# The carry of a recurrent scan kept in fp32, its low part subtracted from SBUF alone

## What is computed

```python
def res_step(prev, xt):
    new = jnp.tanh(xt + prev @ W_res.T)          # W_res is 256 x 256
    new = LEAK * new + (1.0 - LEAK) * prev       # LEAK = 0.95
    return (new, new)
_, res_states = jax.lax.scan(res_step, h0, xin)  # h0: (8 batches, 256)
```

## Time and profile before

| | us |
|---|---|
| median of 3 runs | 635.62 (635.25 to 636.78) |
| the profiled execution: its own time | 634.58 |
| its span, first to last instruction | 632.8 |
| busy: TensorE matmul / VectorE / ScalarE / POOL | 596.5 / 549.2 / 456.4 / 190.8 |

### The profile page before, as it was taken

How to read it: one execution, slowest core, us unless ns; L and a number is a source line. 1 busy time by engine, 2 the same in 40 slices (tenths; PEclk the granted TensorE clock), 3 DMA queues, 4 the chain that set the end, 5 groups by cost and what they waited for, 6 DMA issues and landing times.

```text
span 632.8 us, 28184 instructions
## 1 busy us (share of the span) xinstructions
PE 596.5 (94%) x11015; PEld 475.9 (75%) x11015; DVE 549.2 (87%) x2334; ACT 456.4 (72%) x2244; POOL 190.8 (30%) x427
## 2 busy tenths in 40 slices
PE   7888888999999999999999999999999999999973
PEld 2554454888888888888888888888889888888762
DVE  5789996899888889998999999999777799899985
ACT  5687796677777777777777777777757677677664
POOL 1555364000000000010000000000000488888886
PEclk9999999999999999999999999999999999999997
DMA  6000000000000000000000000000030000000001
GB/s 212 2 2 1 2 1 2 4 4 2 4 4 4 4 3 4 4 4 3 4 4 4 4 2 4 4 4 4 3 70 3 3 18 18 19 16 18 16 20 30
DMA packets 8629, 8.30 MB, mean 13 GB/s; under 512 B 944, under 2 KB 7088, under 8 KB 8496
## 3 DMA queue, kind: packets, MB, share of 16 engines
q1 hardware_dynamic: 8208, 5.51, 3.2%
q10 hardware_dynamic: 288, 0.99, 0.5%
HBM read 3.35 MB, written 2.10 MB: 9 GB/s over the span
## 4 chain that ended last, share of the span: by engine, by line
PE 76%; DVE 9%; issue 5%; ACT 4%; POOL 4%; DMA 1%; POOLq 0%; SPq 0%; DVEq 0%
PE PS L1447 26%; PE PS L1494 15%; PE PS L1649 6%; PE PS L1459 4%; PE PS L1465 4%; PE PS L1396 2%; PE PS L1454 2%; PE PS L1397 2%; PE PS L1403 2%; PE PS L1627 2%; PE PS L1332 2%; PE PS L1371 2%; PE PS L1355 1%; PE PS L1638 1%; PE PS L1383 1%
## 5 line engine op out<-in xcount | busy, mean ns | idle before, releaser
L611 ACT ACTIVATE y<-PS 128x16 f16<-128x16 f32 x512 | 93.8, 183 | 134.3 <-PE PS L1459 129.5
L1494 PE MATMUL PS<-ballast,ident 128*128 128x245 f16 (+6 forms) x661 | 152.2, 301 | 0.0
L1010 DVE TENSOR_TENSOR y_lo<-ys,y 128x16 f16<-128x16 f32 x512 | 97.9, 191 | 44.8 <-ACT ys L612 37.2
L1447 PEld LDWEIGHTS PS<-y,res_hi 128*128 128x128 f16 x2048 | 98.1, 96 | 49.4 <-ACT y L611 16.3
L1447 PE MATMUL PS<-y_lo,res_hi 128*128 128x8 f16 x2048 | 128.1, 168 | 0.2
L1447 PE MATMUL PS<-y,res_hi 128*128 128x8 f16 x2048 | 127.0, 168 | 0.1
L1447 PE MATMUL PS<-y,res_lo 128*128 128x8 f16 x2048 | 123.6, 166 | 0.0
L442 POOL TENSOR_TENSOR small<-small,minus_half 128x2 f32<-128x2 f32 x32 | 22.6, 706 | 311.8 <-DVE y_lo L1010 279.8
L1013 DVE SCALAR_TENSOR_TENSOR kp_lo<-PS,setup,kp 128x16 f16<-128x16 f32 x512 | 114.9, 224 | 0.0
L573 ACT ACTIVATE prob<-PS,exp_up,sc 128x512 f32<-128x512 f32 x128 | 100.3, 790 | 1.5 <-PE PS L1383 1.3
L578 ACT ACTIVATE prob_hi<-PS,exp_up,sc 128x512 f16<-128x512 f32 x128 | 100.6, 792 | 0.0
(11 more groups left out here) (223 smaller groups left out, 1339.0 us busy)
## 6 DMA issues: line engine op xcount, KB each, us to landing
ys<-in_x SPq DMA_DIRECT2D x8, 256.0 KB, 7.7
out<-gate_all SPq DMA_DIRECT2D x24, 64.0 KB, 1.5
mats<-in_mats ACTq DMA_DIRECT2D x1, 709.0 KB, 5.1
h_last<-h_all SPq DMA_DIRECT2D x4, 128.0 KB, 3.1
gate_last<-gate_all SPq DMA_DIRECT2D x4, 128.0 KB, 2.8
out<-gate_last SPq DMA_DIRECT2D x16, 32.0 KB, 1.9
rows<-in_rows ACTq DMA_DIRECT2D x1, 257.5 KB, 7.6
wall<-in_wall SPq DMA_DIRECT2D x1, 256.0 KB, 4.9
```

The costliest lines, as they stand in the source:

```text
L611: a_.activation(y16[:, :].rearrange("p (m b) -> p m b", m=NH), pre, ACT.Tanh, scale=back).then_inc(y16_ready, 1)
L1010: v.tensor_tensor(y_lo[:, :], ys[:, :, bass.ds(i * STEPS + (1 + t), 1)].rearrange("p n o -> p (n o)"), y16[:, :], ALU.subtract).then_inc(l ...
L1447: t_.matmul(dst[:, m, :], wts[:, k, m * P:m * P + P], st[:, k * B:k * B + B], start=False, stop=False, skip_group_check=True)
L1494: t_.matmul(at[:, 0:size], ident16[:, :], ballast[:, 0:size], start=False, stop=True, skip_group_check=True)
```

## The change

The carry is written by ScalarE as fp32 (`kp`). Its high part is no tensor of its own: it is the upper 16 bits of each fp32 word, read as bfloat16 with a stride of two (`kp_hi`). TensorE multiplies it with a copy of the scaled identity in bfloat16 (`carry_id_top`), which VectorE makes once before the scan. VectorE's low part becomes kp - kp_hi, a tensor_tensor with both inputs in SBUF, in all 32 bodies. `kp_lo` stays fp16 and is still multiplied with the fp16 `carry_id`. Waits and semaphores stay as they are.

```diff
-        kp16 = sb("kp16", [P, NH * B], F16)
+        kp = sb("kp", [P, NH * B])
+        kp_hi = kp[:, :].bitcast(BF16).rearrange("p (m b two) -> p m b two", m=NH, two=2)[:, :, :, 1]
...
+        carry_id_top = sb("carry_id_top", [P, P], BF16)
...
-                a_.activation(kp16[:, :].rearrange("p (m b) -> p m b", m=NH), pre, ACT.Copy, scale=keep_scale
+                a_.activation(kp[:, :].rearrange("p (m b) -> p m b", m=NH), pre, ACT.Copy, scale=keep_scale
...
-                v.memset(kp16[:, :], 0.0).then_inc(kp_ready, 1)
+                v.memset(kp[:, :], 0.0).then_inc(kp_ready, 1)
...
             def weights_high():
                 v.tensor_scalar(carry_id[:, :], ident[:, :], setup[:, 25:26], None, ALU.mult)
+                v.tensor_scalar(carry_id_top[:, :], ident[:, :], setup[:, 25:26], None, ALU.mult)
...
                 dve.wait_ge(kp_ready, n + 1)
-                v.scalar_tensor_tensor(kp_lo[:, :].rearrange("p (m b) -> p m b", m=NH), PRE[t % 2][:, r, :, t // 2, :], setup[:, 24:25],
-                                       kp16[:, :].rearrange("p (m b) -> p m b", m=NH), ALU.mult, ALU.subtract
-                                       ).then_inc(kp_lo_ready, 1)
+                v.tensor_tensor(kp_lo[:, :].rearrange("p (m b) -> p m b", m=NH), kp[:, :].rearrange("p (m b) -> p m b", m=NH), kp_hi,
+                                ALU.subtract).then_inc(kp_lo_ready, 1)
...
-                t_.matmul(dst, carry_id[:, :], kp16[:, :].rearrange("p (m b) -> p m b", m=NH), start=False, stop=False,
+                t_.matmul(dst, carry_id_top[:, :], kp_hi, start=False, stop=False,
```

## The result

The changed kernel takes 631.13 us (median of 8 runs, 630.66 to 633.44), the kernel before 635.30 us (8 runs, 634.61 to 636.78). The ratio is 0.9947, 95% interval 0.9936 to 0.9958: faster by 4.2 us, where 9.1 were predicted. The profiled execution of the changed kernel took 632.54 us, 1.4 above its median; its span is 630.8 us.

A forecast was written before the change was run, and what follows sets the result against it. In bodies 0 to 23 a chain of latencies through kp_lo bounds most steps, TensorE the others and most late ones. -13.1 + 0.2 - 1.5 + 5.3 = -9.1 us gave a median of 626.5 us, range 619.5 to 630.5.

The forecast's parts named there:

- Which of the 324 steps can use it: Bodies 0 to 23, steps waiting for kp_lo: 178 with exponentials gain 0.038 us, 146 others 0.043; together -13.1 us.
- rival 2: Steps with exponentials: ScalarE was already the limit, 6.8 us less gain; 633.3 us with lost ties, 628.0 without; chance 0.08.
- kp_lo gets shorter: VectorE's kp_lo takes 0.18 us with both inputs in SBUF, 0.043 us less, its start unmoved.
- What costs nothing: Scan steps: fp32 carry, bfloat16 high-carry matmul at a stride of two, memset and memory add no time.
- rival 3: The strided bfloat16 input leaves kp_lo as slow as before: about 635.6 to 641 us; 0.07 shared with other rivals.
- rival 4: TensorE drains when switching fp16 and bfloat16 each step: about 644 us at 0.1 us; within a shared 0.07.
- The second identity: One extra VectorE instruction before the scan, making carry_id_top: +0.2 us, bounds 0 and 1.26.
- The late bodies: Readout bodies: shorter kp_lo waits in 46 of 128 steps give -1.5 us, contests with POOL cost +5.3 us.
- The ties: Late rounds: kp_lo and POOL's subtraction L529 start together in 23 of 28; kp_lo loses, +0.27 us for a whole tie.
- rival 1: Late bodies: kp_lo wins the ties against POOL, leaving -14.4 us, 621.2 us; chance 0.30.
- The sum: Whole kernel: -13.1 + 0.2 - 1.5 + 5.3 = -9.1 us, predicted median 626.5 us.

The follow-up runs named there:

- run 3: The changed kernel with the exponentials inside the scan over 448 of 512 columns, a timing-only kernel: 627.60 us, ratio 0.9897 to the kernel before.
- run 8: The kernel before plus a 16-column ScalarE copy that nothing reads, in steps 8 to 15 of bodies 0 to 22: 649.70 us, ratio 1.0224.
- run 9: The changed kernel plus a 16-column ScalarE copy that nothing reads, in steps 8 to 15 of bodies 0 to 22: 648.56 us, ratio 1.0203.
- run 2: The changed kernel with kp_lo read from PSUM in all bodies; fp32 carry, bfloat16 high part and second identity stay: 635.50 us, ratio 1.0012.
- run 1: The changed kernel with kp_lo from SBUF in bodies 0 to 24 only, from PSUM in 25 to 31: 626.36 us, ratio 0.9873.
- run 5: The changed kernel with kp_lo from SBUF in bodies 25 to 31 only, from PSUM in 0 to 24: 640.93 us, ratio 1.009.
- run 6: The changed kernel with kp_lo from PSUM only in steps 0 and 1 of each four of bodies 25 to 31: 625.74 us, ratio 0.9856.
- run 7: The changed kernel with a one-column POOL memset between the two subtractions of a readout: 627.12 us, ratio 0.9868.
- run 4: The kernel before with the exponentials inside the scan over 448 of 512 columns, a timing-only kernel: 634.56 us, ratio 0.9999.

## Why the prediction was wrong

- **The step that failed is "Which of the 324 steps can use it".** I took ScalarE's slack in the 178 steps with an exponential as 0.038 us, from 0.70 (exponential to tanh, in the scan) against 0.66 (back to back, before the scan). What it can sustain there is a slack of 0.014: the steps stay at 0.893 (run 3: with shorter exponentials 0.866 at once; runs 8 and 9: the same limit in both kernels). The 0.66 itself was right, for exponentials, which start 0.66 apart before the scan even several in a row, and it is what the first exponential of a body shows here. It left out the three short instructions. They start 0.08, 0.06 and 0.06 us apart, 0.866 in all with the 0.66, but sustained the four take 0.893: if the exponential keeps its 0.66, each short one costs 0.077, about 0.01 more than its start shows, and under load the tanh comes 0.68 to 0.69 behind the exponential (280.39 to 281.08 above). So the term was 178 x 0.014 = 2.5 us, and a little more for the first two steps of each body, where the lead is still there. Summed in the profiles, the steps t = 8 to 15 gave 3.7 us against before and 3.3 against run 2, and not 6.8. The mechanism was right and so was the doubt (rival 2 with a slack of nothing); the truth lay between the two.
- **kp_lo gets shorter.** Right in kind: its start stayed, its wait went. Its duration was mis-sized, 166 ns and not 180; but it could give only what TensorE waited, so the free steps gained 0.041 and not 0.058. All steps of bodies 0 to 23 but those with an exponential gave 5.3 us against before, 5.7 against run 2, where 6.3 were forecast: 146 x 0.041 = 6.0, less some 0.6 because t = 0 is held by the exponential of the step before it.
- **What costs nothing.** Right (run 2): bfloat16 between fp16 matmuls, the fp32 carry, the strided read. Rivals 3 and 4 fall.
- **The second identity.** 0.19 us until the next start, as taken. The first tanh is no sharper test of it: in the profiles of the other kernels it comes anywhere from 112.7 to 114.9 us.
- **The late bodies.** The ties were found and called for POOL, and so it was in 22 rounds, though not in body 25 (runs 1, 5, 6 and 7); rival 1, with a chance of 0.30, falls. The call had some luck in it: it rested on the single row of L968, which started 2 ns ahead, and the edge that I read off, a lead between 0 and 0.02 us, is no edge, since a lead of 5 ns won in body 25. The price was right: 0.27 us net a round in bodies 26 and 27, as forecast for a whole tie. The net came out at +4.8 against +3.8, and the two terms (-1.5 and +5.3) weren't measured apart. The gain was too large: 46 x 0.035 is 1.6 and not 1.5, and in run 6, without the ties, bodies 25 to 30 gave 0.1 us and body 31 0.4.
- **The sum.** -9.0 + 0.3 + 4.8 = -3.9, against -9.1. Of the 5.2 between them the bodies 0 to 23 hold 4.1, the late bodies 1.0, the identity 0.1. The range ended at 630.5, 0.6 short of the result, because it took in only part of rival 2: its upper end with lost ties was 633.3, and I had given it 0.08 on the strength of rows that answered another question.

Not settled: what decides whether the clock falls to 1.2 GHz around the end of the scan. In the profiled executions of before and of runs 1, 3, 4, 5, 6 and 8 it did not, and the end was short (23.1 to 23.2 us); in those of the changed kernel and of runs 2 and 9 it fell, and the end was long (24.8 to 25.0); in run 7 it fell in body 31, and the end was 23.3. No run took that apart. It is open too why kp_lo, a few ns ahead, won in body 25 and lost in the 22 rounds.

**The better version.** Run 6 (625.74 us, 0.9856 of before) and run 1 (626.36, 0.9873) are faster than both kernels, and not to be told from each other: the SBUF source where POOL is quiet, the PSUM source where POOL has its pair of long subtractions. Last starts of the tanh in run 6, for comparison with the two at the top:

```profile
L613 ACT ACTIVATE y<-PS x512: 184/184/218, 114.9 to 600.8; 128x16 f16<-128x16 f32 x171
```

## What to carry to other kernels

Here, moving an operand from PSUM to SBUF took 58 ns off a VectorE instruction of 16 columns, and put that instruction, now with two inputs in SBUF, into a contest with POOL's long subtractions that cost up to 0.33 us each time (0.49 for 0.16). The form can be chosen step by step, so take the short one where POOL is quiet and keep the other where it isn't. Before counting a gain in full, ask for each kind of step which engine is the next limit, and measure that limit by what the engine sustains: from several steps in a row at that limit, or by lengthening the engine's work in the kernel before until the step follows, not from the distance of two starts. In the runs here ScalarE's durations grew, with the work unchanged, only where ScalarE was the bound (the changed kernel, runs 8 and 9), and stayed at 0.18 us where it was not (before, runs 3 and 4): a growing duration is worth a look.

## What the hardware showed that I had not expected

- The recorded duration of ScalarE's tanh, 0.18 us, grew to 0.28 in run 8 and 0.31 in run 9 under a steady overload, with nothing changed in the instruction. I read it as starts that lie 0.10 to 0.13 us ahead of the work.
- Of a VectorE instruction with two SBUF inputs and a POOL instruction that start together, the recorded start doesn't tell who waits. In the changed kernel VectorE was ahead by 1 to 8 ns in 22 rounds and waited each time; ahead by 5 ns in body 25 and by 15 in body 28 (t = 4) it did not wait. Ahead by 35 to 41 ns (run 7) it never did. In run 7's few other rounds it waited when 4, 4, 5 and 10 ns ahead, and didn't at 8 (body 25 again) and at 27; twice, 16 and 8 ns behind, it didn't wait and POOL's instruction was the one drawn out, to 0.50 us, and 19 ns behind it waited. Within some 20 ns the order of the records did not tell here who waits; mostly it was VectorE.
- The Trainium skill, SBUF — State Buffer, section Who interferes with whom, says that the pair of ports that the two engines share goes to whoever issues first, for the whole instruction. The rows agree that the loser waits out the whole instruction (0.49 us for 0.17 of work, ending 0.03 behind POOL's end). That the first wins can't be read from the recorded starts at these distances; whether the issue was in another order than the starts, no run shows.
